# Semaphore clears beside the next stage, node tiles over five groups of edges, and final stores in two parts, in a one-core graph, expert and LSTM kernel

## The reference, cut to what matters

```python
msg = h_all[edge_type, src] / deg[edge_type, dst][:, None]   # h_all = x @ W_r, per relation
x = x + segment_sum(msg, dst) + x @ W0_w.T + W0_b             # of layernorm(x)
x = x + ffn(layernorm(x))      # 8 experts 256-1024-256, one for each token, capacity 1.25 T / 8
h = layernorm(x) @ W
out = segment_sum(norm[:, None] * h[src], dst) + b            # with self loops
x = x + leaky_relu(out, 0.2)
x_proj = einsum('btd,gd->btg', layernorm(x), W_ih) + b_ih + b_hh
# LSTM over the 6250 rows, then logits, argmax g, running sums of g * lstm_out
x = x + 2.0 * lstm_out + prefix * fw_att + suffix * bw_att    # the output, 6250 x 256
```

## Time and profile before

| | us |
|---|---|
| median of 3 runs | 4646.22 (4645.78 to 4651.95) |
| profiled execution, its time | 4647.93 |
| its span, first to last instruction | 4646.2 |
| PE busy | 3767.1 (81%) |
| DVE busy | 1840.3 (40%) |
| Pool busy | 1642.8 (35%) |
| ACT busy | 889.8 (19%) |
| mean granted clock of TensorE | 0.865 |

### The profile page before, as it was taken

The page is one execution under the profiler, slowest core; times in us unless marked ns, Lnnn a source line. Parts: engine busy times, 40 slices in busy tenths (PEclk is TensorE's granted clock), DMA queues, the critical chain, the costliest instruction groups (busy, mean ns, idle before and its releaser), DMA issues. The chain is left out here.

```text
span 4646.2 us, 64849 instructions
## 1 busy us (share of the span) xinstructions
PE 3767.1 (81%) x19849; PEld 2867.8 (62%) x19850; DVE 1840.3 (40%) x5512; ACT 889.8 (19%) x2492; POOL 1642.8 (35%) x1753
## 2 busy tenths in 40 slices
PE   3999999977788878776999765666777777999993
PEld 1444454467777777654656545555555557999993
DVE  3444410033434343362112373233444543444684
ACT  0333333300000000041111170000000002444452
POOL 1000000067777777521000137777777750000000
PEclk9999999978877787757999886688888898999996
DMA  4323333333334333322222144344455544433331
GB/s 151 125 116 126 119 128 145 148 108 109 109 111 110 111 110 111 93 77 85 71 75 75 40 148 135 111 127 134 148 155 166 173 143 138 149 113 115 105 110 74
DMA packets 213029, 545.40 MB, mean 117 GB/s; under 512 B 42697, under 2 KB 111158, under 8 KB 197919
## 3 DMA queue, kind: packets, MB, share of 16 engines
q1 hardware_dynamic: 124496, 302.44, 19.3%
q0 software_dynamic: 83376, 235.38, 17.4%
q10 hardware_dynamic: 4896, 4.46, 0.3%
HBM read 363.19 MB, written 178.51 MB: 117 GB/s over the span
## 5 line engine op out<-in xcount | busy, mean ns | idle before, releaser
L724 POOL DMA_INDIRECT a_msg<-scratch_hrel,k_rel_row x784 | 753.2, 961 | 1080.6 <-issue 1075.1
L1488 POOL DMA_INDIRECT b_msg<-scratch_gtab,k_src_row x784 | 770.4, 983 | 271.1 <-issue 262.0
L658 PE MATMUL r_psm<-k_w,r_xnT 128*128 128x512 f32 x1568 | 741.4, 609 | 0.9 <-ACT r_xnT L601 0.9
L827 PE MATMUL a_ps<-a_hit,a_msg 128*128 128x128 f32 x3136 | 566.3, 355 | 182.9 <-DMA a_msg<-scratch_hrel,k_rel_row 179.2
L1537 PE MATMUL b_ps<-b_hit,b_msg 128*128 128x128 f32 x3136 | 511.7, 332 | 206.2 <-DMA b_msg<-scratch_gtab,k_src_row 199.6
L827 PEld LDWEIGHTS a_ps<-a_hit,a_msg 128*128 128x128 f32 x3136 | 525.5, 262 | 217.0 <-DVE a_hit L766 139.4
L1537 PEld LDWEIGHTS b_ps<-b_hit,b_msg 128*128 128x128 f32 x3136 | 479.6, 241 | 250.4 <-issue 166.7
L1912 PE MATMUL l_psg<-k_hall,k_whhT 128*128 128x128 f32 x4672 | 565.9, 279 | 5.7 <-DVE k_hall L2029 5.4
L1912 PEld LDWEIGHTS l_psg<-k_hall,k_whhT 128*128 128x128 f32 x4672 | 543.2, 193 | 13.3 <-DVE k_hall L2029 5.9
L658 PEld LDWEIGHTS r_psm<-k_w,r_xnT 128*128 128x128 f32 x1568 | 278.1, 191 | 273.7 <-issue 251.9
L610 ACT COPY r_hst<-r_psm 128x512 f32<-128x512 f32 x392 | 229.5, 586 | 518.2 <-PE r_psm L658 518.1
(11 more groups left out here) (255 smaller groups left out, 3845.6 us busy)
## 6 DMA issues: line engine op xcount, KB each, us to landing
scratch_hrel<-r_hst SPq DMA_DIRECT2D x98, 1024.0 KB
l_xr<-scratch_xrow SPq DMA_DIRECT2D x146, 512.0 KB, 3.6
scratch_xrow<-n_xs SPq DMA_DIRECT2D x50, 512.0 KB, 3.3
a_msg<-scratch_hrel,k_rel_row POOLq DMA_INDIRECT x784, 2.8
b_msg<-scratch_gtab,k_src_row POOLq DMA_INDIRECT x784, 2.8
scratch_buf<-k_zpad POOLq DMA_DIRECT2D x8, 1024.0 KB, 6.5
x_xr<-scratch_buf SPq DMA_DIRECT2D x8, 1024.0 KB, 6.5
x_w1s<-in_L_ffn_w_dram SPq DMA_DIRECT2D x8, 1024.0 KB, 10.7
```

The costliest lines, as they stand in the source:

```text
L658: mm = pe.matmul(psm[:, c % 4], xnT[:, u, kk], k.w[:, kk, c * 512:(c + 1) * 512], start=(kk == 0), stop=(kk == 1))
L724: pool.indirect_dma_start(msg[:, q, j], None, table, bass.IndirectOffsetOnAxis(ap=rows[:, g, j:j + 1].bitcast(U32), axis=0)).then_inc(s_m[ ...
L827: mm = pe.matmul(ps[:, u, kk, 0:WIN], msg[:, q % SL, j, kk * P:(kk + 1) * P], hit[:, u, j], start=(j == 0), stop=(j == PER - 1))
L1488: pool.indirect_dma_start(msg[:, q, j], None, k.gtab, bass.IndirectOffsetOnAxis(ap=k.src_row[:, g, j:j + 1].bitcast(U32), axis=0)).then_in ...
```

## The change

Six edits. `end_stage` resets Pool's queue once and clears semaphores by ranges of adjacent numbers, one instruction for each range, with no barrier behind; the semaphores are given back one stage later, so that the next stage takes others, and Pool's DMA semaphores alternate between two banks. All Blocks are opened with a flag that leaves out Pool's drain at their end (the block's own barrier stays). `for_windows` ends without a barrier. The gather clears its own semaphores only in its windowed form, and the LSTM's opening sweep leaves that to the branch for more sweeps, which isn't taken. A node tile's pieces are spread over the slots `first[t]` to `first[t] + 5`, the projection's two halves in different slots. Each final store is two: 112 partitions and 13.

```diff
     def end_stage(self):
-        clear(self, self.stage_sems + self.pool_dma_sems)
-        for sem in self.stage_sems:
+        self.nc.gpsimd.dma_reset()
+        nums = sorted(sem.num for sem in self.stage_sems + self.pool_banks[self.stage % 2][0:self.pool_dma_used])
+        first = 0
+        for i in range(1, len(nums) + 1):
+            if i == len(nums) or nums[i] != nums[i - 1] + 1:
+                self.nc.gpsimd.sem_clear(range(nums[first], nums[i - 1] + 1))
+                first = i
+        for sem in self.ended_sems:
             self.nc.release_semaphore(sem)
-        self.stage_sems = []
+        self.ended_sems, self.stage_sems = self.stage_sems, []
         self.pool_dma_used = 0
+        self.stage += 1
...
-    with nc.Block() as block:
+    with nc.Block(no_gpsimd_drain=True) as block:
...
         else:
             fixed()
-    nc.all_engine_barrier()
...
-            clear(k, sems)
+            if fixed is not None:
+                clear(k, sems)
...
-            slots = range(first[-1] + 3)
+            slots = range(first[-1] + 6)
...
+                        for t in begun(g - 4):
+                            project(t, 1)
+                        for t in begun(g - 3):
+                            project(t, 0)
                         for t in begun(g - 2):
-                            project(t)
-                        for t in begun(g - 1):
                             turn(t)
                         for t in begun(g):
                             turn_sums(t)
...
                     for g in slots:
+                        for t in begun(g - 2):
+                            turn(t)
                         for t in begun(g - 1):
-                            turn(t)
-                        for t in begun(g):
                             root(t)
...
+                        for t in begun(g - 5):
+                            projected(t, 1)
+                        for t in begun(g - 4):
+                            projected(t, 0)
                         for t in begun(g - 2):
-                            projected(t)
+                            norm(t)
                         for t in begun(g - 1):
-                            norm(t)
-                        for t in begun(g):
                             rows(t)
...
-                    sp.dma_start(out3[:, a:b], k.x3s[0:CU, a:b]).then_inc(S["st"], 16)
-                sp.wait_ge(S["st"], 16 * len(chunks))
+                    for lo, hi in ((0, CU // 16 * 16), (CU // 16 * 16, CU)):
+                        sp.dma_start(out3[lo:hi, a:b], k.x3s[lo:hi, a:b]).then_inc(S["st"], 16)
+                sp.wait_ge(S["st"], 16 * 2 * len(chunks))
...
-            clear(k, sems)
+            if not opening:
+                clear(k, sems)
         sweep([(WARM, False), (0, True), (0, True)], True)
         with nc.If(nc.values_load(flag[0:1, 0:1], min_val=0, max_val=1) > 0):
+            clear(k, sems)
             with nc.Fori(0, C - 1):
```

More of the change, by code:

```diff
@@ L1556, in turn, with project @@
                         mm.then_inc(S["t2"], 1)
-                    def project(t):
+                    def project(t, h):
                         pe.wait_ge(S["xt"], t + 1)
[L1560 to L1567, removed]
+                        if t >= 1:
+                            pe.wait_ge(S["ev"], 2 * t + h - 1)
+                        for kk in range(2):
+                            mm = pe.matmul(psm[:, h], xT[:, t % 2, kk],
+                                           wT[:, kk, 4 * h:4 * h + 4].rearrange("p g d -> p (g d)"),
+                                           start=(kk == 0), stop=(kk == 1))
+                        mm.then_inc(S["pm"], 1)
                     pe.wait_ge(S["w"], 16 * 5)
```

19 lines of the change are left out of this document (9 added, 10 removed).

## The result

The changed kernel takes 4543.43 us in the median of 4 runs (4540.85 to 4544.71), the kernel before 4646.00 (4 runs, 4639.29 to 4651.95). The ratio is 0.9779, with a 95% interval of 0.9762 to 0.9796: 2.2% faster, 102.6 us. The prediction said 4549 (4536 to 4572). The profiled execution's span is 4539.1 us, 107.1 less than before; some 5 of these are how far the two profiled executions lie on different sides of their medians.

The account below looks back on a forecast made before the run. TensorE is busy 81% of 4646.2 us, but the gains were to lie between stages and at two tails: boundaries 41.0, stores 31.3 and tiles 25 make 97.3 us, so 4549 us from the 4646.22 median, range 4536 to 4572.

Parts of the forecast that it names:

- Boundaries: Between stages: SP's barrier waits behind single clears, for_windows's barriers and Pool's block-end drains go or are hidden, 41.0 us (36 to 44).
- the 32.6: Between stages, without the drain flag: 31.6 us from clears and their barriers, 1.0 from the barrier ending for_windows.
- the 8.4: Pool's drain at block ends: 3.5 us at the first graph stage, 4.06 at routing, 0.79 at the experts.
- Rival A: Between stages: the reset's drain takes over the plain drain's time, 9.3 us come back, 4558 us in all; chance 0.15.
- Final stores: At the program's end: splitting each store into 112 and 13 partitions uses more DMA engines, gaining 31.3 us (29 to 34).
- My other bound: Final stores: at the rate of 128-partition stores, 347 GB/s and share 0.84, 6.4 MB take 18.4 us.
- the prediction's own sign: Final stores: an end later than 20 us behind their first store would show the prediction wrong.
- Rival C: Final stores: the 13 rows go to one engine, stores end near 4623, gain 10 us, 4570 in all; chance 0.06.
- Tiles: Last graph stage: node tiles spread over five groups let PE follow gather landings and shorten the tail, 25 us (18 to 28).
- The 18 x 1.4 us: Last graph stage: each of 18 PE waits for n_xn loses 1.4 us beyond spare time, making the 25 us lag.
- B: Last graph stage: the lag moves rather than goes; 4561 us if half stays, 4574 if all; chance 0.12.
- D: Last graph stage: TensorE's clock stays at 1.2 GHz once PE catches up, losing up to 189 us, 4738; chance 0.03.

## Why the prediction was right, step by step

*Boundaries: 41.0 forecast, 41.3 measured.* Right in size and place: the kernel with the drains kept has the 32.6 of it, the one with the drains back misses the 8.4. Two reasons in the prediction were wrong, though. I had the plain drain last as long as Pool's last instructions take to be retired; the kernel with only the flag shows 7.9 us begun 71 us after the last gather's issue. And I added the flag's gain to that of the barriers as if each stood alone; alone it gives nothing, since the barrier's drain takes its place. The sum was right because the change takes away both. Rival A didn't come, with or without a plain drain ahead: a reset takes 0.27 to 0.29 us in all eight places.

*Final stores: 31.3 forecast (29 to 34), 26.8 measured.* The mechanism was right and the row's price was mis-sized: 0.38 us a row, read where five engines write, is about 0.5 where sixteen do. My other bound, 347 GB/s over a share of 0.84, I took at 347 (18.4 us and an end by 4604); with the 320 GB/s measured, 6.4 MB take 20 us, and 2.8 of start and landing make the 22.8. By the prediction's own sign (an end more than 20 us behind the first store) this term was wrong. Its 0.3 us for the issue of a store, hidden behind DVE, was wrong too: the median is 1.7 us and the last store goes out 4.7 us behind the additions.

The Trainium skill, "DMA: Bandwidth & Descriptors", section "Where 436 GB/s comes from", has the 358 GB/s. As an estimate by it the stores end at 4583.1 + 2 + 17.9 = 4603.0, which is 1.6 us behind my 4601.4 and not within 1 us, as I wrote, and 2.9 short of the 4605.9 that 22.8 us make. The traces show 320 GB/s for this transfer and, in ten us of the one of 112 rows, 364. Rival C is out: 13 rows on one engine would have been 38 us or more.

*Tiles: 25 forecast (18 to 28), 31.1 measured.* The lag went from 25.0 to 3.3 us (forecast 1). Pool's first to last issue became 4.0 us shorter (1008.1 to 1004.1), as it waited less for PE to free buffers; I had called its pace untouched. The tail behind the last sums is 18.0 us (3765.30 to 3783.32), where I had 21 to 23. The step that failed is the cause: "because DVE makes it behind its own wait for both halves of the projection". The timeline leaves that wait 0.4 of the 3.4 us; the rest is the chain of rows with one group's sums as its only cover (the kernel with the sums ahead cuts the waits to 1.1 us). The change moves `turn` a group further from `turn_sums`, which covers the same chain.

The 18 x 1.4 us that made the 25.0 of lag were luck in part. Measured from each group's last gather plus 2.8 us to its first product, the lag of the kernel before is 3.3 us at group 152 and grows to 25.0 at the last, by 21.7: 1.2 us for each of 18 tiles. (8.4 of work and a wait of 3.40 are more than the 11.2 that two groups took, since PE's passes overlap.) In the changed kernel it lies between 0.0 and 3.3 us from group 100 on. So a lag of up to 3 us belongs to either kernel, and the forecast 1 us was too little by that much.

*Rivals.* B didn't come: PE's waits for n_xT and for n_xn in the last stretch are 0.7 us each in all. D neither: PE waits for gathers now, and the granted clock from 3600 to 3700 is 0.91, near the 0.90 from 3700 to 3800 before:

```profile
3600.00:3700.00 100.00, 78.10 (x418) 58.15 (x419) 53.19 (x119) 5.34 (x16) 76.23 (x79) 0.91 0.58 178
```

So two of the three parts lie outside their own ranges, 4.5 too much and 6.1 too little, and that they all but cancel is luck. The rest of the difference between 4549 and 4543.43, some 4 us, is below what a run tells.

## What to carry to other kernels

Here a drain on Pool cost more the more Pool had issued before it, and it was paid at the first drain that came, a barrier's too: take out all of them or put a queue reset ahead, and look at each line's drains by minimum and maximum, not at the sum. When PE waits for another engine, count what PE's own list holds between the instruction that feeds the chain and the one that needs it; moving long work into that space costs no more slots. A time per row taken where few DMA engines run is a floor, not a price, for all sixteen. And look at how long the issuing instructions themselves take: when they grow, the engine that issues falls behind the one that computes.

## What the runs showed of the hardware that was not expected

- Pool's plain drain takes 7.90 us behind 784 gathers, 4.06 behind 49 indirect transfers (routing's writes and the combining's gathers alike) and 0.79 behind the relations and the experts, to within 0.02 us in all runs on both kinds of chip, and no less 71 us later. What it waits for isn't shown, since it doesn't pass with time.
- A row of 10,240 bytes from SBUF to HBM takes 0.38 us an engine with five engines writing, and in windows of ten us 0.45 to 0.52 on average with sixteen, where the median row still takes 0.385. Which resource the sixteen share wasn't tried.
- SP's instructions that issue these stores take 0.26 to 0.40 us at first, but from the fourth of ten on 1.2 to 2.5 us in the changed kernel, and 2.4 for the last of five before. What they wait for isn't shown.
- A chip on which the same program takes 8% longer, nearly all of it in stages with indirect transfers, by gaps in Pool's issue that the trace doesn't explain. What stalls it stays open.
